# Gates of the gated recurrence: the narrow layers moved between the z products, gate input and last gate layer joined by group, the next attention opened later

## The chip, the cores and the metric

The kernel runs as one program on one core of a Trainium2 chip. The time is the device time of one execution in microseconds. The kernel before took 1679.32 us as the median of three runs (1677.64 to 1679.97). The lines below are of one more execution, taken by the hardware profiler.

The core's engines each have their own queue of instructions and meet only at semaphores. TensorE (PE) multiplies and writes to PSUM, which has eight banks of 128 partitions by 2 KB. ScalarE (ACT) and VectorE (DVE) read PSUM and write to the on-chip memory SBUF. GpSimd (POOL) works on SBUF, and SyncE (SP) issues the DMAs.

## What is computed

Four layers stand one behind the other, on x of 16 sequences of 100 tokens with 256 features and a context of 16 sequences of 361. Layer 0 is a self attention, a cross attention and an MLP with layer norms; layer 1 has two attentions, each with a gated MLP. Layer 2 holds the part that is changed, and layer 3 attends to the context again. Of layer 2, cut to what matters here:

```python
x_norm = _rms(x, norm1_scale)
q = x_norm @ Wq + bq
k = x_norm @ Wk + bk
v = x_norm @ Wv + bv
z = x_norm @ Wz + bz
gamma_base = jax.nn.sigmoid(jax.nn.gelu(z @ Wg1 + bg1) @ Wg2 + bg2)
gamma_mod = jax.nn.sigmoid(jax.nn.gelu(k @ Wgc1 + bgc1) @ Wgc2 + bgc2)
gamma = jnp.clip(gamma_base * gamma_mod, 1e-06, 1.0 - 1e-06)

def step(h_prev, zt_gt):
    z_t, g_t = zt_gt
    gate = jax.nn.sigmoid(z_t @ Wgz + bgz + h_prev @ Wgh + bgh)
    h_tilde = (1.0 - gate) * h_prev + gate * z_t
    h_t = h_tilde + g_t * h_prev
    return (h_t, h_t)
```

The recurrence runs over the 100 tokens. Beside it, the same layer attends with 8 heads from q to the context (mem_k and mem_v are the context), and adds h, the attention's output and 0.1 v.

## The kernel before, in words

Features lie on the partitions, tokens on the free axis: 16 sequences are four groups g of 4, and a group is N = 400 columns. 256 features are two halves m. So a product of one group is one [128 x 400] tile of PSUM for each half, and a weight of 256 x 256 takes two matrix products per half. On TensorE each fp32 product of 400 columns shows as two matmul records; a pair of halves is eight records (x8).

The stages are s0, c0, f0 (layer 0), s1, f1, c1, f2 (layer 1), then the gates, then c2 (the attention of layer 2, with the 100 steps of the recurrence woven in), ft and layer 3. The order on each engine is written out by hand: `program_pe`, `program_act`, `program_dve`, `program_pool` call the same stages, and generators that yield at each slot ("fill", "opening", "step") are advanced with `next` at fixed places, at the same places on every engine. Waits are computed from marks, so an instruction waits for what it reads and for what must be free, and no more.

The stage of the gates is `pe_gates`, `act_gates` and `dve_gates`. Names in it:

- z: the product x_norm Wz (line 777 calls `pe_products`, whose matmuls are line 405); ScalarE adds the bias and writes zs (line 1185).
- ga: the two narrow layers z Wg1 and x_norm (Wk Wgc1), 64 outputs each, side by side in one bank (lines 789 and 790); ScalarE applies the gelu (line 1189, tile GH, which lies in probs).
- gz: the gate input z Wgz (line 793); ScalarE writes it to t (T2, two buffers), and VectorE splits it into three bf16 parts (lines 1624 to 1631, "split").
- gA and gB: the last gate layers (line 801), four matmuls a group; ScalarE applies the sigmoid (lines 1201 and 1202), VectorE multiplies, clips and adds one (lines 1637, 1640, 1643, "gm").
- the opening: what the attention c2 needs before its first sequence (`pe_open`, lines 588 to 612). In slots: two query products q, the keys of sequence 0 (one slot and an empty one), then three slots with the values v of a key chunk and a product "tops" (line 488) whose maxima VectorE takes (line 1343), one with tops alone, the keys of sequence 1 (and an empty slot), and the turn of the maxima (line 496). That makes 11 slots.

The stage runs in three loops over g: all z; then ga, gz and one slot of the opening for each g; then gA, gB and two slots for each g. On VectorE the second loop is the splits, the third the gm's, each with the opening's maxima in the same slots.

PSUM is given out by rings that remember who frees each bank: `flow` (banks 0 to 5) for z, ga, gz, gA and gB, a ring of banks 4 and 6 for q, v and the turn of c2, and pairs (0,1) and (2,3) for keys and tops. A take on TensorE waits for the reader of that bank's last use:

```python
if b + i in freed:
    if due(freed[b + i]):
        pe.wait_ge(producer(freed[b + i]), at(freed[b + i]))
freed[b + i] = point
```

Behind the gates, ScalarE waits for the last gm (line 1208) before it goes on, and GpSimd's first step of the recurrence waits for it too (line 1820). The first step on TensorE (lines 821 and 828) waits for the last split and the last gB, and the first scores R0 (lines 515 and 518) wait for the maxima's rows (line 1354).

## Time and profile before

| | us |
|---|---|
| median of three runs | 1679.32 |
| lowest, highest | 1677.64, 1679.97 |
| time of the profiled execution | 1679.33 |
| its span, first to last instruction | 1677.6 |
| PE busy | 1583.5 (94%) |
| DVE busy | 775.7 (46%) |
| ACT busy | 673.0 (40%) |
| POOL busy | 257.2 (15%) |

The span is 1.73 us shorter than the time of the same execution; the rest lies around it. TensorE is busy nearly all the time, so the places of interest are the few where it isn't. The stage of the gates runs from 1121 to 1190 us of the span. The granted clock of TensorE is a mean of 0.96 of full speed over the whole span.

### The profile page before, as it was taken

To read this page: it belongs to the slowest core of one execution; us is meant where nothing else is said; L and a number is where in the kernel's file an instruction comes from. 1 tells how busy PE (TensorE), PEld (TensorE's weight loads), DVE (VectorE), ACT (ScalarE), POOL (GpSimd) and SP (SyncE) were. 2 spreads that over 40 slices of the span, in tenths; PEclk is the share of its full clock that TensorE was granted. 3 is DMA by queue.
4 is the path that set the end of the run, shared out by engine and by line. 5 is a ranking of instruction groups with operands and counts; after the bars stand their busy time and mean duration, and the time that the engine had idled before them with its cause. 6 is when DMAs were issued, how large, how long until landed. Compare 5 with 4: busy or idle time off the path is not lost.

```text
span 1677.6 us, 30686 instructions
## 1 busy us (share of the span) xinstructions
PE 1583.5 (94%) x13224; PEld 1028.4 (61%) x13224; DVE 775.7 (46%) x1568; ACT 673.0 (40%) x1417; POOL 257.2 (15%) x446
## 2 busy tenths in 40 slices
PE   7998899999999999999999999998899999979998
PEld 6655456666665556555677765553677777645565
DVE  1567767667552245311233332235465566552132
ACT  2455446556454433111234422234453444333343
POOL 1333301010000000000022210000243344320000
PEclk9899989999899999999999999999798799889999
DMA  4211000000000010000100000000000000011021
GB/s 149 97 46 37 19 26 2 2 2 2 2 5 22 0 76 1 19 1 0 76 1 1 1 26 0 0 7 1 26 2 2 2 2 2 2 37 38 0 90 57
DMA packets 19272, 36.97 MB, mean 22 GB/s; under 512 B 2016, under 2 KB 17344, under 8 KB 17856
## 3 DMA queue, kind: packets, MB, share of 16 engines
q1 hardware_dynamic: 19136, 35.01, 6.3%
q8 instruction: 104, 1.70, 0.4%
q14 instruction: 32, 0.26, 0.0%
HBM read 33.36 MB, written 1.64 MB: 21 GB/s over the span
## 4 chain that ended last, share of the span: by engine, by line
PE 84%; DVE 10%; ACT 5%; issue 1%; DMA 0%; SPq 0%; DVEq 0%; ACTq 0%
PE psum L405 37%; PE psum L729 10%; PE psum L518 8%; PE psum L450 8%; PE psum L550 6%; PE psum L488 2%; DVE maxima L1343 2%; PE psum L515 2%; PE psum L828 2%; ACT probs L1026 2%; DVE denoms L1381 1%; PE psum L856 1%; PE psum L869 1%; DVE q_then_o L1386 1%; PE psum L821 1%; PE psum L837 1%
## 5 line engine op out<-in xcount | busy, mean ns | idle before, releaser
L1343 DVE TENSOR_REDUCE maxima<-psum 100x2 f32<-100x722 f32 (+3 forms) x332 | 243.9, 758 | 115.9 <-PE psum L488 95.0
L405 PE MATMUL psum<-x_resid,weights 128*128 128x400 f32 x832 | 292.8, 502 | 4.0 <-ACT probs L1026 1.8
L1026 ACT ACTIVATE probs<-psum 128x800 f32<-128x800 f32 (+3 forms) x240 | 171.7, 747 | 148.8 <-PE psum L518 146.7
L405 PEld LDWEIGHTS psum<-x_resid,weights 128*128 128x128 f32 x832 | 155.7, 190 | 120.3 <-issue 4.3
L729 PE MATMUL psum<-weights 128*128 128x400 f32 x512 | 175.0, 499 | 0.7 <-DVE maxima L1343 0.7
L405 PE MATMUL psum<-weights,ctx_t 128*128 128x256 f32 (+1 forms) x576 | 162.4, 407 | 2.4 <-ACT weights L947 1.7
L450 PE MATMUL psum<-ctx_t,weights 128*128 128x361 f32 x384 | 146.2, 508 | 3.1 <-ACT probs L947 1.3
L729 PEld LDWEIGHTS psum<-weights 128*128 128x128 f32 x512 | 97.2, 190 | 75.1 <-DVE maxima L1343 0.8
L515 PE MATMUL psum<-max_rows,ones_bf 32*128 32x200 bf16 (+7 forms) x1152 | 132.1, 237 | 9.3 <-ACT probs L1026 5.6
L997 ACT ACTIVATE values<-psum 128x256 f32<-128x256 f32 (+2 forms) x176 | 67.5, 384 | 150.9 <-PE psum L405 115.8
L405 PEld LDWEIGHTS psum<-weights,ctx_t 128*128 128x128 f32 (+1 forms) x576 | 101.6, 190 | 41.7 <-issue 9.8
L947 ACT ACTIVATE weights<-psum 128x400 f32<-128x400 f32 (+2 forms) x80 | 38.0, 475 | 210.4 <-PE psum L405 210.3
L550 PE MATMUL psum<-probs,values 128*32 128x100 f32 (+5 forms) x3328 | 115.7, 259 | 0.4 <-DVE q_then_o L1399 0.2
L518 PE MATMUL psum<-q_then_o,keys 32*128 32x100 f32 (+4 forms) x1280 | 109.7, 298 | 0.0
L1773 POOL TENSOR_TENSOR q_masked_bf<-q_then_o,ones 128x200 bf16<-128x200 f32 x48 | 25.5, 535 | 502.8 <-ACT q_then_o L947 439.4
L550 PEld LDWEIGHTS psum<-probs,values 128*32 128x32 f32 (+5 forms) x3328 | 87.7, 117 | 24.1 <-issue 20.9
L1567 DVE TENSOR_TENSOR weights<-psum,weights 128x400 f32<-128x400 f32 x64 | 36.7, 574 | 138.3 <-PE psum L405 120.0
L518 PE MATMUL psum<-q_masked,keys 32*128 32x200 f32 (+2 forms) x1024 | 99.5, 350 | 0.0
L450 PEld LDWEIGHTS psum<-ctx_t,weights 128*128 128x128 f32 x384 | 72.2, 201 | 43.6 <-issue 12.2
L518 PEld LDWEIGHTS psum<-q_then_o,keys 32*128 32x128 f32 (+4 forms) x1280 | 96.0, 191 | 3.0 <-issue 0.5
L947 ACT ACTIVATE weights<-psum,vectors 128x400 f32<-128x400 f32 x80 | 46.3, 592 | 111.4 <-PE psum L405 102.8
L515 PEld LDWEIGHTS psum<-max_rows,ones_bf 32*128 32x128 bf16 (+5 forms) x1152 | 67.1, 120 | 33.3 <-DVE maxima L1343 11.3
(151 smaller groups left out, 2238.2 us busy)
## 6 DMA issues: line engine op xcount, KB each, us to landing
weights<-in_w SPq DMA_DIRECT2D x2, 3072.0 KB, 9.6
staged<-in_ctx SPq DMA_DIRECT2D x32, 128.0 KB, 2.1
values<-in_ctx SPq DMA_DIRECT2D x32, 128.0 KB, 2.2
weights<-in_w SPq DMA_DIRECT2D x3, 1024.0 KB, 4.8
weights<-in_src SPq DMA_DIRECT2D x1, 2368.0 KB, 13.4
weights<-in_w SPq DMA_DIRECT2D x1, 2048.0 KB, 7.8
weights<-in_tw SPq DMA_DIRECT2D x2, 1024.0 KB, 4.8
staged<-in_ctx SPq DMA_DIRECT2D x16, 105.0 KB, 2.1
```

Source lines behind the costliest of these rows:

```text
L405: i = nc.tensor.matmul(PS[0:rows, bk, 0:n], lhs, rhs, start=k == 0, stop=k == len(terms) - 1)
L450: i = nc.tensor.matmul(PS[:, bk + m, 0:C], w(WN[t][1], c, m * P, (m + 1) * P), CT[:, b, c, :], start=c == 0, stop=c == DC - 1)
L488: i = nc.tensor.matmul(PS[0:S, bk + d, 0:C], queries_bf(t, b, i0 + d, c, e), keys_bf(t, b, i0 + d, c), start=True, stop=True)
L515: nc.tensor.matmul(PS[0:kn, bk + d, m * n:(m + 1) * n], ONEB[tile_rows(t, i0 + d), 0:kn], MB[tile_rows(t, i0 + d), b % 2, c * n:(c + 1) * ...
L518: i = nc.tensor.matmul(PS[0:kn, bk + d, m * n:(m + 1) * n], keys_of(t, b, i0 + d, c, k0, kn), queries_of(t, b, i0 + d, c), start=False, st ...
L550: mm = nc.tensor.matmul(PS[tile_rows(t, i), bk, o:o + S], lhs, probs_of(t, b, i, c, kc, kn, e), start=kc == 0, stop=kc == lastk)
L729: i = nc.tensor.matmul(PS[:, bk, 0:N], w(wd, k, m * P, (m + 1) * P), hidden[:, k, :], start=k == 0, stop=k == 7)
L947: nc.scalar.activation(out, PS[0:rows, bank(use), 0:n], func, **kw).then_inc(act_results, mark("act", point or f"{use} out"))
L997: nc.scalar.activation(dst, src, ACT.Copy).then_inc(act_results, mark("act", f"{use} out"))
L1026: nc.scalar.activation(PT[0:kn, k % PROBS_KEPT, :, 0:n], PS[0:kn, bk:bk + 2, 0:n], ACT.Exp).then_inc(act_results, mark("act", f"{t} p{b} { ...
L1343: nc.vector.reduce_max(top, src, AX).then_inc(dve_results, mark("dve", f"{t} m{b} {j}"))
L1567: nc.vector.tensor_tensor(H[:, m, :], PS[:, bank(up), 0:N], U[:, m % 2, :], ALU.mult).then_inc(dve_results, mark("dve", f"{of} u{g} {m}"))
```

## The change

The amount of work stays the same; its order changes, on TensorE, ScalarE and VectorE alike.

1. The narrow layers ga of group g - 1 follow the z products of group g; those of the last group follow gz of group 0 (`pe_gate_downs`).
2. The second and the third loop become one: gz of g, then gA and gB of g, and on VectorE the split of g, then gm of g.
3. The table OPEN_AT says how many slots of the opening are advanced: none in the loop of z; after gz of group g 0, 1, 2, 4; after gA and gB of group g 0, 1, 4, 1. So no slot is used at group 0, both queries come at group 1, the keys of sequence 0 and all values and tops at group 2, and the keys of sequence 1 and the turn at group 3, ahead of its gA and gB.
4. VectorE advances both numbers of a group at once, between its split and its gm.

```diff
--- before.py
+++ after.py
@@ -150,6 +150,8 @@
 AFTER = {"f0": "c0", "f1": "s1", "f2": "c1", "ft": "c2"}
 NORM_AFTER = {"f0": "n3", "f2": "r1"}
 TAIL_AT = 10
+
+OPEN_AT = ((0, 0, 0, 0), (0, 1, 2, 4), (0, 1, 4, 1))
 OPENS = {"f0": "s1", "f1": "c1"}
 PROBS_KEPT = 6
 ROUND_AT = {}
@@ -580,6 +582,10 @@
             for _ in itertools.zip_longest(*parts):
                 yield
 
+        def advance(part, slots):
+            for _ in range(slots):
+                next(part, None)
+
         def later(slots, part):
             for _ in range(slots):
                 yield
@@ -764,6 +770,17 @@
             for m in range(DC):
                 pe_products(pe, lin[""], f"bias {name}{m}", f"bias {name}{m} out", [(w(ww, k, m * P, (m + 1) * P), vec(bv, k)) for k in range(DC)], n=1)
 
+        def pe_gate_downs(pe, g):
+
+            for m in range(DC):
+                if due(f"z{g} {m} out"):
+                    pe.wait_ge(act_results, at(f"z{g} {m} out"))
+            bk = flow.take(pe, f"ga{g}", f"ga{g} out")
+            for k in range(DC):
+                nc.tensor.matmul(PS[0:64, bk, 0:N], w("wg1", k, 0, 64, 64), seq("zs")[:, k, cols(g)], start=k == 0, stop=k == DC - 1)
+                i = nc.tensor.matmul(PS[64:P, bk, 0:N], w("k2", k, 0, 64, 64), XN[g][:, k, :], start=k == 0, stop=k == DC - 1)
+            i.then_inc(products_ready, mark("pe", f"ga{g}"))
+
         def pe_gates(pe):
 
             opening = pe_open(pe, "c2")
@@ -780,19 +797,15 @@
                     if due("w c2"):
                         pe.wait_ge(producer("w c2"), at("w c2"))
                     pe_bias(pe, "o2", "awo", "abv")
+                else:
+                    pe_gate_downs(pe, g - 1)
+                advance(opening, OPEN_AT[0][g])
             for g in range(NG):
                 for m in range(DC):
-                    if due(f"z{g} {m} out"):
-                        pe.wait_ge(act_results, at(f"z{g} {m} out"))
-                bk = flow.take(pe, f"ga{g}", f"ga{g} out")
-                for k in range(DC):
-                    nc.tensor.matmul(PS[0:64, bk, 0:N], w("wg1", k, 0, 64, 64), seq("zs")[:, k, cols(g)], start=k == 0, stop=k == DC - 1)
-                    i = nc.tensor.matmul(PS[64:P, bk, 0:N], w("k2", k, 0, 64, 64), XN[g][:, k, :], start=k == 0, stop=k == DC - 1)
-                i.then_inc(products_ready, mark("pe", f"ga{g}"))
-                for m in range(DC):
                     pe_products(pe, flow, f"gz{g} {m}", f"gz{g} {m} out", [(w("gz", k, m * P, (m + 1) * P), seq("zs")[:, k, cols(g)]) for k in range(DC)])
-                next(opening, None)
-            for g in range(NG):
+                if g == 0:
+                    pe_gate_downs(pe, NG - 1)
+                advance(opening, OPEN_AT[1][g])
                 if due(f"ga{g} out"):
                     pe.wait_ge(act_results, at(f"ga{g} out"))
                 for m in range(DC):
@@ -800,8 +813,7 @@
                         bk = flow.take(pe, f"{name}{g} {m}", f"{name}{g} {m} out")
                         nc.tensor.matmul(PS[:, bk, 0:N], WT[rows, WAT[ww] + m * P:WAT[ww] + (m + 1) * P], GH[rows, g, :],
                                          start=True, stop=True).then_inc(products_ready, mark("pe", f"{name}{g} {m}"))
-                next(opening, None)
-                next(opening, None)
+                advance(opening, OPEN_AT[2][g])
             for _ in opening:
                 pass
 
@@ -1185,23 +1197,25 @@
                     act_evac(act, f"z{g} {m}", seq("zs")[:, m, cols(g)], bias=vec("bz", m))
                 if g == 0:
                     act_root(act, "r1", NG - 1)
+                else:
+                    act_evac(act, f"ga{g - 1}", GH[:, g - 1, :], func=ACT.Gelu_apprx_tanh, bias=vec("d_gates"))
+                advance(opening, OPEN_AT[0][g])
             for g in range(NG):
-                act_evac(act, f"ga{g}", GH[:, g, :], func=ACT.Gelu_apprx_tanh, bias=vec("d_gates"))
                 given = f"gz split{g - 2}" if g >= 2 else f"r1 t{NG - 2 + g} 1"
                 if due(given):
                     act.wait_ge(dve_results, at(given))
                 for m in range(DC):
                     act_evac(act, f"gz{g} {m}", T2[:, g % 2, m, :], bias=vec("d_gz", m))
-                next(opening, None)
-            for g in range(NG):
+                if g == 0:
+                    act_evac(act, f"ga{NG - 1}", GH[:, NG - 1, :], func=ACT.Gelu_apprx_tanh, bias=vec("d_gates"))
+                advance(opening, OPEN_AT[1][g])
                 if g >= 2:
                     if due(f"gm{g - 2}"):
                         act.wait_ge(dve_results, at(f"gm{g - 2}"))
                 for m in range(DC):
                     act_evac(act, f"gA{g} {m}", seq("gms")[:, m, cols(g)], func=ACT.Sigmoid, bias=vec("bg2", m))
                     act_evac(act, f"gB{g} {m}", SG[:, g % 2, m, :], func=ACT.Sigmoid, bias=vec("bgc2", m))
-                next(opening, None)
-                next(opening, None)
+                advance(opening, OPEN_AT[2][g])
             for _ in opening:
                 pass
             if due(f"gm{NG - 1}"):
@@ -1617,6 +1631,7 @@
             nc.vector.memset(HP[:, :, :, :], 0.0).then_inc(dve_results, mark("dve", "hp0"))
             mark_same("h-1", "hp0")
             mark_same("wp2", "hp0")
+            advance(opening, sum(OPEN_AT[0]))
             for g in range(NG):
                 if due(f"gz{g} 1 out"):
                     dve.wait_ge(act_results, at(f"gz{g} 1 out"))
@@ -1629,8 +1644,7 @@
                 if due(f"gz rest {g}"):
                     dve.wait_ge(dve_results, at(f"gz rest {g}"))
                 nc.vector.tensor_tensor(parts[:, :, 2, :], gz, parts[:, :, 1, :], ALU.subtract).then_inc(dve_results, mark("dve", f"gz split{g}"))
-                next(opening, None)
-            for g in range(NG):
+                advance(opening, OPEN_AT[1][g] + OPEN_AT[2][g])
                 if due(f"gB{g} 1 out"):
                     dve.wait_ge(act_results, at(f"gB{g} 1 out"))
                 gm = seq("gms")[:, :, cols(g)]
@@ -1641,8 +1655,6 @@
                 if due(f"clip{g}"):
                     dve.wait_ge(dve_results, at(f"clip{g}"))
                 nc.vector.tensor_scalar(gm, gm, 1.0, None, ALU.add).then_inc(dve_results, mark("dve", f"gm{g}"))
-                next(opening, None)
-                next(opening, None)
             for _ in opening:
                 pass
 
```

In the rows of order below, x4 means four instructions alike, and what an instruction waits for stands in brackets. The changed file has 12 lines more above this place, so its line numbers are higher.

TensorE, the end of the gates, before, from the last tops (line 488) to the first step of the recurrence (821). Line 801 is gA and gB, 450 the keys of sequence 1, 496 the turn:

```order
L488 MATMUL psum<-keys_bf,q_masked_bf 100x361 [waits dve_results]
L488 MATMUL psum<-keys_bf,q_masked_bf 100x361
L801 MATMUL psum<-probs,weights 128x400 [waits dve_results]
L801 MATMUL psum<-probs,weights 128x400 x3
L450 MATMUL psum<-ctx_t,weights 128x361 [waits act_results]
L450 MATMUL psum<-ctx_t,weights 128x361 x3
L801 MATMUL psum<-probs,weights 128x400 x4
L496 MATMUL psum<-constants,maxima 128x100
L821 MATMUL psum<-weights,ident_bf 128x96 [waits act_results]
```

The same place in the changed kernel: 490 is tops, 407 on weights the gate input gz of the last group, 452 the keys of sequence 1, 498 the turn, 814 gA and gB:

```order
L490 MATMUL psum<-keys_bf,q_masked_bf 100x361 [waits dve_results]
L490 MATMUL psum<-keys_bf,q_masked_bf 100x361
L490 MATMUL psum<-keys_bf,q_masked_bf 100x361 [waits dve_results]
L490 MATMUL psum<-keys_bf,q_masked_bf 100x361
L407 MATMUL psum<-weights 128x400 [waits dve_results]
L407 MATMUL psum<-weights 128x400 x3
L452 MATMUL psum<-ctx_t,weights 128x361 [waits act_results]
L452 MATMUL psum<-ctx_t,weights 128x361 x3
L498 MATMUL psum<-constants,maxima 128x100 [waits dve_results]
L814 MATMUL psum<-probs,weights 128x400 x4
L833 MATMUL psum<-weights,ident_bf 128x96 [waits act_results,dve_results]
```

The gA and gB of group 2 no longer stand between the tops and the keys; gz of group 3 does. Only one set of gA and gB is left behind the tops, and it follows the turn. The tops and gz wait for VectorE's maxima.

VectorE, from the last split to the start of the second gm, before. Lines 1624 to 1631 are a split, 1637 to 1643 a gm, 1343 the maxima:

```order
L1624 CAST weights<-t 128x2x400 [waits act_results]
L1627 TENSOR_TENSOR weights<-t,weights 128x2x400 [waits dve_results]
L1628 TENSOR_TENSOR t<-t,weights 128x800
L1631 TENSOR_TENSOR weights<-t,weights 128x2x400 [waits dve_results]
L1637 TENSOR_TENSOR weights<-weights,probs 128x2x400 [waits act_results]
L1640 TENSOR_SCALAR weights<-weights 128x2x400 [waits dve_results]
L1643 TENSOR_SCALAR weights<-weights 128x2x400 [waits dve_results]
L1343 TENSOR_REDUCE maxima<-psum 100x2 [waits products_ready] x2
L1637 TENSOR_TENSOR weights<-weights,probs 128x2x400 [waits act_results]
```

The same engine in the changed kernel, from the split of group 2 (1639 to 1646) over all maxima (1357) and the gm of group 2 (1651 to 1657) to the split of group 3:

```order
L1639 CAST weights<-t 128x2x400 [waits act_results]
L1642 TENSOR_TENSOR weights<-t,weights 128x2x400 [waits dve_results]
L1643 TENSOR_TENSOR t<-t,weights 128x800
L1646 TENSOR_TENSOR weights<-t,weights 128x2x400 [waits dve_results]
L1357 TENSOR_REDUCE maxima<-psum 100x2 [waits products_ready] x4
L1651 TENSOR_TENSOR weights<-weights,probs 128x2x400 [waits act_results]
L1654 TENSOR_SCALAR weights<-weights 128x2x400 [waits dve_results]
L1657 TENSOR_SCALAR weights<-weights 128x2x400 [waits dve_results]
L1639 CAST weights<-t 128x2x400 [waits act_results]
```

Before, the splits of all groups come ahead of the first gm, and that gm ahead of the first maxima. Now two gm's are done by then, and the maxima stand ahead of the third.

ScalarE, before, from the z of group 1 on. A result in weights is zs or a sigmoid, one in probs is a gelu or a sigmoid, one in t is gz:

```order
L947 ACTIVATE weights<-psum,vectors 128x400 [waits products_ready] x6
L947 ACT_TABLE_LOAD
L947 ACTIVATE probs<-psum,vectors 128x400 [waits products_ready]
L947 ACTIVATE t<-psum,vectors 128x400 [waits products_ready] x2
L947 ACTIVATE q_then_o<-psum,vectors 128x400 [waits products_ready]
L947 ACTIVATE probs<-psum,vectors 128x400 [waits products_ready]
```

In the changed kernel:

```order
L959 ACTIVATE weights<-psum,vectors 128x400 [waits products_ready] x2
L959 ACT_TABLE_LOAD
L959 ACTIVATE probs<-psum,vectors 128x400 [waits products_ready]
L959 ACTIVATE weights<-psum,vectors 128x400 [waits products_ready] x2
L959 ACTIVATE probs<-psum,vectors 128x400 [waits products_ready]
L959 ACTIVATE weights<-psum,vectors 128x400 [waits products_ready] x2
L959 ACTIVATE probs<-psum,vectors 128x400 [waits products_ready]
L959 ACTIVATE t<-psum,vectors 128x400 [waits products_ready] x2
L959 ACTIVATE probs<-psum,vectors 128x400 [waits products_ready]
L959 ACT_TABLE_LOAD
L959 ACTIVATE weights<-psum,vectors 128x400 [waits products_ready]
```

The table of the gelu is loaded behind the second group's z. The table of the sigmoid is loaded behind the last gelu, as before; what now follows that gelu at once is the first sigmoid.

## Rows read from the trace of the kernel before

**Rows 1.** Page, the chain that ended last, shares of the span by engine

```profile
PE 84%; DVE 10%; ACT 5%; issue 1%; DMA 0%; SPq 0%; DVEq 0%; ACTq 0%
```

**Rows 2.** Windows: start:end, length; busy (records) of PE, PEld, DVE, ACT, POOL; clock; DMA; GB/s

```profile
1134.00:1158.00 24.00, 22.21 (x80) 10.18 (x79) 10.91 (x12) 11.62 (x19) 1.82 (x2) 1.00 0.00 1
1158.00:1187.00 29.00, 20.65 (x68) 9.63 (x66) 13.09 (x17) 13.18 (x25) 0.00 (x0) 0.76 0.00 0
1166.00:1170.00 4.00, 2.65 (x8) 1.18 (x8) 2.11 (x3) 0.92 (x2) 0.00 (x0) 0.66 0.00 0
1194.00:1198.00 4.00, 3.21 (x32) 2.51 (x31) 2.21 (x10) 1.21 (x3) 0.90 (x5) 0.50 0.00 0
1360.00:1380.00 20.00, 19.63 (x254) 13.81 (x250) 10.58 (x38) 6.95 (x21) 5.36 (x13) 1.00 0.01 2
1420.00:1440.00 20.00, 20.00 (x201) 15.14 (x201) 9.69 (x36) 6.91 (x21) 6.95 (x15) 0.58 0.00 1
```

**Rows 3.** Timeline of TensorE: start, duration in us; in brackets idle before, releaser

```profile
1129.85 5.54 PE L405 MATMUL psum<-staged,weights 128*128 128x400 f32 x16
1135.32 0.55 PE L789 MATMUL psum<-weights 128*64 128x400 f32 x1
...
1136.81 2.95 PE L405 MATMUL psum<-weights 128*128 128x400 f32 x8
...
1151.90 2.70 PE L450 MATMUL psum<-ctx_t,weights 128*128 128x361 f32 x8 [0.69 <-ACT t L947]
...
1162.74 1.13 PE L405 MATMUL psum<-weights,ctx_t 128*128 128x256 f32 x4 [1.04 <-ACT weights L947]
...
1163.80 0.35 PE L488 MATMUL psum<-keys_bf,q_masked_bf 32*100 32x361 bf16 x2
...
1167.35 3.04 PE L801 MATMUL psum<-probs,weights 64*128 64x400 f32 x8 [1.85 <-DVE maxima L1343]
...
1179.72 4.94 PE L450 MATMUL psum<-ctx_t,weights 128*128 128x361 f32 x8 [1.25 <-ACT probs L947]
...
1184.59 1.61 PE L801 MATMUL psum<-probs,weights 64*128 64x400 f32 x8
...
1187.73 0.34 PE L821 MATMUL psum<-weights,ident_bf 128*128 128x96 bf16 x1 [1.29 <-ACT probs L947]
...
1190.25 0.21 PE L515 MATMUL psum<-max_rows,ones_bf 32*128 32x100 bf16 x2 [1.60 <-DVE max_rows L1354]
```

**Rows 4.** Groups by line, TensorE: busy us, mean ns, idle before and its releasers

```profile
L801 PE MATMUL psum<-probs,weights 64*128 64x400 f32 x32 | 9.3, 716 | 4.8 <-DVE maxima L1343 4.8
```

**Rows 5.** Timeline of VectorE in the gates

```profile
1140.43 0.58 DVE L1624 CAST weights<-t 128x800 bf16<-128x800 f32 x1 [6.55 <-ACT t L947]
...
1142.97 0.99 DVE L1631 TENSOR_TENSOR weights<-t,weights 128x800 bf16<-128x800 f32 x1
...
1166.39 1.72 DVE L1343 TENSOR_REDUCE maxima<-psum 100x2 f32<-100x722 f32 x2
...
1187.70 0.99 DVE L1637 TENSOR_TENSOR weights<-weights,probs 128x800 f32<-128x800 f32 x1 [5.88 <-ACT probs L947]
...
1189.34 0.58 DVE L1643 TENSOR_SCALAR weights<-weights 128x800 f32<-128x800 f32 x1
...
1190.11 0.25 DVE L1655 TENSOR_REDUCE scan_state<-psum 128x32 f32<-128x96 f32 x1
```

**Rows 6.** Timeline of ScalarE in the gates

```profile
1136.04 1.28 ACT L947 ACT_TABLE_LOAD   x1
1137.33 0.59 ACT L947 ACTIVATE probs<-psum,vectors 128x400 f32<-128x400 f32 x1
...
1185.62 0.59 ACT L947 ACTIVATE weights<-psum,vectors 128x400 f32<-128x400 f32 x1
...
1187.07 0.60 ACT L947 ACTIVATE probs<-psum,vectors 128x400 f32<-128x400 f32 x1
```

**Rows 7.** Timeline of GpSimd in the gates

```profile
1147.54 1.82 POOL L1773 TENSOR_TENSOR q_masked_bf<-q_then_o,ones 128x200 bf16<-128x200 f32 x2 [162.11 <-ACT q_then_o L947]
```

## The prediction

> **What bounds the kernel now.** I read the page first: the chain that ended last lies on TensorE for 84% of the span and on VectorE and ScalarE for 15% [rows 1]. So the change matters where TensorE waits or runs slowly. Then I cut the stage of the gates into windows [rows 2]. From 1134 to 1158 us TensorE is busy 22.21 of 24 us at clock 1.00; from 1158 to 1187 it is busy 20.65 of 29 us at clock 0.76. The second loop is nearly dense, the third isn't. The timeline of TensorE [rows 3] and its groups [rows 4] say why. The matmuls of gA and gB wait 4.8 us in all for VectorE's maxima; once it is 1.85 us, at 1167.35. The order says what those maxima stood behind: the last split and the first gm. The maxima free the bank pairs that the next gA needs, so TensorE waits for work of VectorE that it does not need itself. In those waits the clock falls: 0.66 from 1166 to 1170 with TensorE busy 2.65 of 4 us [rows 2]. At 1.2 GHz eight records of gA and gB take 3.04 us and not 1.61, and the keys' eight 4.94 and not 2.70 [rows 3].
>
> What ends last in the stage is a chain over three engines. TensorE ends the last gB at 1184.59 + 1.61 = 1186.2; ScalarE's last sigmoid ends at 1187.07 + 0.60 = 1187.67 [rows 6]; the last gm runs from 1187.70 to 1189.34 + 0.58 = 1189.92 [rows 5]; the first sum of the recurrence starts at 1190.11, and the first scores R0 at 1190.25, after 1.60 us of waiting for the maxima's rows [rows 3].
>
> **What the same work needs without waits.** The change adds and removes no matmul, evacuation, vector operation or DMA, and it leaves the number of table loads alone: the order shows one for the gelu and one for the sigmoid. So I price TensorE's work from 1135.32, where the z products end before, each group at clock 1.00 [rows 3]:
> - four narrow layers at 1136.81 - 1135.32 = 1.49: 5.96
> - four gz at the price of a z pair, (1135.32 - 1129.85) / 2 = 2.74: 10.96
> - two queries, half of that, 1.37: 2.74
> - two times keys at 2.70: 5.40
> - three v at 1163.80 - 1162.74 = 1.06: 3.18
> - four tops and the turn at 0.35 (the turn has no row here; it is one transpose, and I give it the price of tops): 1.75
> - four times gA and gB at 1.61: 6.44
>
> Sum 36.4, so that the last gB could end at 1171.75. It ends at 1186.2. Of the 14.5 us between, 4.8 are the waits of [rows 4], 0.69, 1.04 and 1.25 are three other waits of [rows 3], 2 x (3.04 - 1.61) = 2.9 (two of the four sets of gA and gB ran so) and 4.94 - 2.70 = 2.2 are the slow clock. The rest, 1.6, is smaller gaps that I don't list. All the z come in the same place as before; the three narrow layers between them run in banks long free, and each follows the z of a later group, so that ScalarE has had 2.74 us for an evacuation of 0.59 us [rows 6]. No wait there.
>
> **The waits that the new order brings.** I walked the three queues with the rings of banks.
> - gA of group 1 takes the bank of the query just issued, and waits until ScalarE has emptied it. The keys at 1151.90 waited 0.69 for just such an evacuation [rows 3]. I take 0.7.
> - The first v waits for the first sigmoid of group 2, which stands behind four evacuations of keys. The v before waited 1.04 at 1162.74 [rows 3], with a table load in front; without one I get 0.2. Bounds 0 and 1.04.
> - gz of group 3 takes the pair of the third tops and waits for their maxima. v with tops takes 1.06 + 0.35 = 1.41, a maximum 1.72 / 2 = 0.86 [rows 5], so VectorE keeps up, and only the last one shows: 0.86. I take 0.9. Bound below 0, above 1.85, the wait in [rows 3].
> - The keys of sequence 1 take the pair of gz and wait for both its evacuations: 0.7 again.
> - The turn waits for the fourth maximum, done long before (gz and keys, 5.4 us, lie between), and behind the turn stand gA and gB of group 3. Nothing.
> - The masks of GpSimd, 1.82 us for two [rows 7], start when the second query is out; before the first tops there lie gz, keys and gA with gB, 2.74 + 2.70 + 1.61 = 7 us. Nothing.
>
> Sum 2.5, so the last gB ends at 1174.25. Behind it the pieces are those of before in the same order: ScalarE has keys to empty, then four sigmoids, and ends 1187.67 - 1186.2 = 1.47 later: 1175.7. The last gm takes 1189.92 - 1187.70 = 2.22: 1177.95. The maxima's rows now lie ahead of it, so the first sum starts at 1178.0, and not at 1190.11. That is 12.1 us less.
>
> Is VectorE free enough? Its first split can start when gz of group 0 is emptied: 1135.32 + 3 x 1.49 + 2.74 + 0.75 = 1143.3, 2.9 later than the 1140.43 of before. From there it has four splits of 1142.97 + 0.99 - 1140.43 = 3.53, four gm of 2.22, four maxima of 0.86 [rows 5], and one operation for the maxima's rows that I give 0.86 too, an upper bound: 27.3. It would be done at 1170.6, 7.4 us ahead of the end I found. It has that much to spend on waits; a wait of 5.88 stood ahead of the last gm before [rows 5].
>
> What follows moves as a whole: the recurrence and R0 start from the last gm, the last split, the maxima's rows and the last sigmoid, and all come 12 us earlier. No load is late: the next weights (f1 of the tail) are issued when the last gB ends, as before, and are wanted only behind the whole of c2.
>
> A rule of the Trainium skill, ScalarE: Activation LUTs, section What ACT_TABLE_LOAD costs, speaks against part of this: it gives 1283 ns for the load plus about 1380 ns of drain for a switch. In this trace the load takes 1.28 us and the activation behind it starts 0.01 us after its end, 1136.04 + 1.28 against 1137.33 [rows 6], so no drain stands behind the load. By the rule the sigmoids of group 0 would come 1.38 us later, the first query's evacuation some 0.5 later, and the gain would be an estimated 11.6; by the rows it is 12.1.
>
> **The sum.** The span is 1677.6 and the same execution's time 1679.33, which is the median's 1679.32 within 0.01; 1.73 us lie around the span. 1677.6 - 12.1 + 1.73 = 1667.2 us. For this case alone I give 1665.5 to 1669.
>
> **The rivals.**
> - *The clock falls inside the new order.* It fell before with TensorE busy 2.65 of 4 us. In the new order it is busy 36.4 of 38.9 us, 94%, as in the dense window (22.21 of 24, 93%, clock 1.00) [rows 2]; but the tops and their maxima stand close together, and the waits of 0.9 and 0.7 with them. If it falls at the third tops, gz (2.74 x (4.94 / 2.70 - 1) = 2.3), keys (2.2) and gA with gB (1.4) grow: 5.9 lost, gain 6.2, 1673.1 us.
> - *The clock stays up at the start of c2.* From 1194 to 1198 it is 0.50 with TensorE busy 3.21 of 4 us [rows 2], after the waits ahead of the first scores. Those are shorter now. At full clock the 3.21 would be 1.6, over ten us of such a stretch 4.0; the steps' chain over VectorE and ScalarE does not quicken, so 2 to 3. Gain 14.6, 1664.7 us.
> - *The change doesn't do what it says.* The maxima were put ahead of gm and gz behind maxima, so the chain third maximum, gz, wait, keys, turn, gA with gB, sigmoids, gm (2.74 + 0.7 + 2.70 + 0.35 + 1.61 + 1.47 + 2.22 = 11.8) ends the stage. I have the third maximum end at 1166.2. If VectorE's queue (split, gm, split, gm, split, four maxima) gets there only at 1178, nothing is gained: 1679 us. For it: VectorE's two kinds of work now alternate, each waiting for ScalarE. Against: 7.4 us of slack, and each group's data are there 3 us or more ahead.
> - *Slower: the slow clock spreads in c2.* From 1420 to 1440 the clock is 0.58 and TensorE gets through 201 records; from 1360 to 1380 at 1.00 it is 254, in both cases busy nearly all of 20 us [rows 2]. Such a stretch costs (254 - 201) / 254 x 20 = 4.2 us. The stage starts 12 us earlier and meets the clock's changes elsewhere. It decides from three more such stretches on (12.6, against a gain of 12.1); with four it is 1684 us. Against: the three runs differ by only 2.33 us, less than one stretch.
>
> **How the numbers follow.** The forecast 0.58, clock falls in the gates 0.18, clock stays up 0.12, other sizes of the same gain 0.04, no gain 0.05, slower 0.03. A measurement of this kernel can tell about 0.2%, 3.4 us, from no change. The first four are faster: 0.92; same 0.05; slower 0.03. The range 1663.5 to 1673.5 takes in both cases of the clock and the bounds of the four waits (1.0 less, or 1.8 more).
>
> **What would show it.** In the changed profile, the last gB should end near 1174, the last gm near 1178, and the first scores follow without a wait for the maxima's rows. The waits of gA and gB for maxima (4.8) should be gone, and one of about 0.9 stand ahead of the last gz. The clock should be 1.00 from 1134 to 1174, with eight records of gA and gB at 1.61 in all groups. The splits should start near 1143, and the sigmoid's table be loaded once. I am wrong if the last gm ends after 1184, if the sigmoids trail TensorE by much more than 1.5 us, or if the time between the first sum and the end of the span grows by more than 3 us.

## The result, and the profile after

| | before | after |
|---|---|---|
| median of 4 runs, us | 1678.48 | 1661.22 |
| lowest, highest | 1677.62, 1679.97 | 1659.63, 1662.4 |
| profiled execution: time, span | 1679.33, 1677.6 | 1661.62, 1659.9 |
| mean granted clock of TensorE | 0.960 | 0.966 |

The changed kernel takes 0.9896 of the time before, 95% interval 0.9878 to 0.9913: faster by 17.3 us. I had forecast 12.1 us less and a range down to 1663.5, so the direction was right and the size was not: 5 us more came than the walk through the gates gives, and 1661.22 lies below the range.

To see where the time went, cut both spans at three marks: VectorE's first scaling of v2 (the first operation behind the norm), the first of the hundred sums of the recurrence and the last of them.

| us | before | after | difference |
|---|---|---|---|
| start to first scaling of v2 | 1130.4 | 1129.5 | -0.9 |
| gates: to the first sum | 59.7 | 47.7 | -12.0 |
| c2: to the hundredth sum | 292.6 | 288.0 | -4.6 |
| rest of the span | 194.9 | 194.7 | -0.2 |

Two rows give the last three marks: VectorE's sums by their line, with least, median and longest duration in ns, then the start of the first and of the last. Before:

```profile
L1655 DVE TENSOR_REDUCE scan_state<-psum x100: 246/257/259, 1190.1 to 1482.7; 128x32 f32<-128x96 f32 x100
```

After:

```profile
L1667 DVE TENSOR_REDUCE scan_state<-psum x100: 247/258/259, 1177.2 to 1465.2; 128x32 f32<-128x96 f32 x100
```

So the gates came out as worked out, and the rest of the gain lies in c2, whose instructions the change does not touch. First the page of after, busy time and the shares of the chain:

```profile
PE 1574.6 (95%) x13224; PEld 1023.7 (62%) x13224; DVE 774.5 (47%) x1568; ACT 673.4 (41%) x1417; POOL 257.3 (16%) x446
PE 84%; DVE 10%; ACT 4%; issue 1%; DMA 0%; SPq 0%; POOL 0%; DVEq 0%; ACTq 0%; POOLq 0%
```

TensorE has the same 13224 records and is busy 8.9 us less (1583.5 before): the same work ran at a higher clock for part of the time. Its gate layers as one group, to set beside [rows 4]:

```profile
L814 PE MATMUL psum<-probs,weights 64*128 64x400 f32 x32 | 7.0, 525 | 0.7 <-ACT q_then_o L959 0.7
```

The mean record fell from 716 to 525 ns, the idle time before the group from 4.8 us behind maxima to 0.7 behind a query. TensorE's timeline over the second half of the new order, beside [rows 3] (start, length, engine, line, operation, wait in brackets):

```profile
1150.18 1.61 PE L814 MATMUL psum<-probs,weights 64*128 64x400 f32 x8 [0.68 <-ACT q_then_o L959]
...
1158.38 2.11 PE L814 MATMUL psum<-probs,weights 64*128 64x400 f32 x8
...
1165.52 2.95 PE L407 MATMUL psum<-weights 128*128 128x400 f32 x8 [0.97 <-DVE maxima L1357]
1169.25 2.67 PE L452 MATMUL psum<-ctx_t,weights 128*128 128x361 f32 x8 [0.78 <-ACT t L959]
1171.76 0.25 PE L498 MATMUL psum<-constants,maxima 100*128 100x100 f32 x1
1171.94 1.61 PE L814 MATMUL psum<-probs,weights 64*128 64x400 f32 x8
1175.16 0.34 PE L833 MATMUL psum<-weights,ident_bf 128*128 128x96 bf16 x1 [1.61 <-ACT probs L959]
```

The four waits that I had put at 0.7, 0.2, 0.9 and 0.7 are 0.68, 0.50 (inside the 2.11 of group 2: eight records alone take 1.61), 0.97 and 0.78, 2.9 us against 2.5. The last gB ends at 1173.55, for 1174.25 in the forecast, with the stage starting 0.9 earlier. The closing stretch on VectorE, beside [rows 5]:

```profile
1164.55 1.73 DVE L1357 TENSOR_REDUCE maxima<-psum 100x2 f32<-100x722 f32 x2 [0.42 <-PE psum L490]
...
1172.59 0.36 DVE L1368 TENSOR_TENSOR max_rows<-psum,constants 128x200 bf16<-128x200 f32 x1
1175.05 0.99 DVE L1651 TENSOR_TENSOR weights<-weights,probs 128x800 f32<-128x800 f32 x1 [2.11 <-ACT probs L959]
1176.08 0.58 DVE L1654 TENSOR_SCALAR weights<-weights 128x800 f32<-128x800 f32 x1
1176.69 0.58 DVE L1657 TENSOR_SCALAR weights<-weights 128x800 f32<-128x800 f32 x1
1177.18 0.25 DVE L1667 TENSOR_REDUCE scan_state<-psum 128x32 f32<-128x96 f32 x1
```

VectorE now waits 2.11 us for the last sigmoid, and its row of maxima was ready long before. The first scores start at 1175.93, without a wait for that row. Last, the clock by windows (length, busy time and records of PE, PEld, DVE, ACT and POOL, then the granted clock, DMA share, GB/s), two of the gates and then c2:

```profile
1134.00:1158.00 24.00, 23.32 (x86) 11.28 (x82) 12.71 (x16) 13.81 (x25) 1.46 (x2) 1.00 0.00 1
1158.00:1174.00 16.00, 13.80 (x55) 7.03 (x53) 11.52 (x15) 8.67 (x19) 0.00 (x0) 1.00 0.00 1
1177.20:1214.78 37.58, 35.51 (x409) 26.53 (x406) 20.64 (x82) 17.22 (x47) 15.31 (x36) 0.78 0.02 7
1245.09:1288.86 43.77, 42.47 (x499) 30.97 (x499) 23.29 (x85) 15.32 (x45) 13.92 (x33) 0.81 0.01 2
1288.86:1320.06 31.20, 30.45 (x468) 23.40 (x467) 21.57 (x83) 15.15 (x45) 13.93 (x33) 1.00 0.01 2
1402.57:1417.98 15.41, 15.30 (x245) 12.01 (x245) 11.36 (x43) 7.80 (x23) 7.45 (x17) 1.00 0.01 3
1438.35:1465.23 26.88, 26.14 (x365) 20.78 (x368) 15.10 (x59) 9.21 (x29) 9.51 (x24) 0.68 0.01 2
1177.20:1465.20 288.00, 278.26 (x3828) 209.42 (x3828) 181.98 (x679) 125.61 (x367) 116.27 (x274) 0.91 0.01 3
```

The stretches of c2 are cut at the same steps of the recurrence in both kernels: 0 to 12, 24 to 36, 36 to 48, 78 to 84, 90 to 99, then the whole. The same of before:

```profile
1190.10:1225.70 35.60, 34.13 (x425) 26.06 (x426) 21.16 (x81) 17.15 (x47) 15.25 (x36) 0.86 0.01 5
1256.02:1297.18 41.16, 39.69 (x499) 28.86 (x499) 23.91 (x84) 15.19 (x45) 13.90 (x33) 0.88 0.01 2
1297.18:1335.36 38.18, 37.54 (x468) 28.64 (x467) 21.52 (x82) 15.35 (x45) 13.88 (x33) 0.78 0.01 2
1417.87:1440.28 22.41, 22.41 (x245) 17.27 (x247) 11.34 (x42) 8.00 (x23) 7.45 (x17) 0.62 0.00 1
1460.65:1482.64 21.99, 19.64 (x362) 15.38 (x365) 15.37 (x58) 9.18 (x29) 9.48 (x24) 1.00 0.01 3
1190.10:1482.70 292.60, 281.92 (x3848) 212.03 (x3852) 183.31 (x680) 125.82 (x367) 116.00 (x274) 0.91 0.01 2
```

Steps 0 to 12 take 2.0 us more after, 24 to 36 take 2.6 more, 36 to 48 take 7.0 less, 78 to 84 take 7.0 less, 90 to 99 take 4.9 more: together 4.5 less, of c2's 4.6. In each pair of rows the records agree within 5% and the longer one has the lower clock. The steps in between (12 to 24, 48 to 78, 84 to 90) take the same time in both to 0.02 us. Of the 4.6 us, 3.7 are busy time of TensorE (281.92 to 278.26) and 0.9 idle time. The change moved the places at which TensorE runs at its lower level, 1.2 GHz, and in before they lie where they cost more.

### The profile page after: what moved, and what is told of

It reads as the page before. It is cut to its first block, busy times and chain, and to the rows that moved or that the text cites. A ratio compares the mean times of both kernels' runs of the same rounds, so it can differ in the third digit from the quotient of the medians.

```text
span 1659.9 us, 30691 instructions
## 1 busy us (share of the span) xinstructions
PE 1574.6 (95%) x13224; PEld 1023.7 (62%) x13224; DVE 774.5 (47%) x1568; ACT 673.4 (41%) x1417; POOL 257.3 (16%) x446
## 4 chain that ended last, share of the span: by engine, by line
PE 84%; DVE 10%; ACT 4%; issue 1%; DMA 0%; SPq 0%; POOL 0%; DVEq 0%; ACTq 0%; POOLq 0%
PE psum L407 38%; PE psum L735 10%; PE psum L520 8%; PE psum L452 8%; PE psum L552 6%; PE psum L490 2%; DVE maxima L1357 2%; PE psum L517 2%; PE psum L840 2%; ACT probs L1038 2%; DVE denoms L1395 1%; PE psum L868 1%; PE psum L881 1%; DVE q_then_o L1400 1%; PE psum L833 1%; PE psum L849 1%
```

## The experiments

They ask two things: which part of the change makes the 12 us, and why c2, untouched, got shorter. Kernels are named by what they change; each table entry below is of the profiled execution unless it says median. The ratio and its 95% interval are estimated from all runs of a comparison, with before measured beside them, and need not be the quotient of the medians.

### Both kernels again

No edit. Was the c2 of each kernel an accident of one execution?

> The kernel before, unchanged, as a second measurement. The change gained 17.3 us of median where I had worked out 12.1; its stage of the gates gave just that 12.1, the rest came from c2, the attention behind the gates. Theory A (the clock's slow stretches in c2 lie elsewhere from execution to execution, and the four runs of each kernel happened to differ): this kernel's c2, from the first sum of the recurrence to the hundredth, will be 3 us or more off the 290 of the first profile, or the median more than 2 us off 1678.5. Theory B (how the gates end decides how c2 runs, the same way in each execution): first sum near 1190, c2 within 1.5 us of the first profile, median 1677.5 to 1680.

> The changed kernel, unchanged, with more runs. Its gates gained 12.0 us, the median 17.3; joined loops with an early opening gained 9.3 in the gates and 15.7 in the median, the late opening alone 13.8 and 21.0. Theory A (the slow stretches of c2 are drawn anew in each execution and the rest of the gain is chance of few runs): with more runs the median moves to 1664 or above, 1678.4 less 12.1 being 1666.3, and the runs spread over 10 us or more, as those of the kernel before do (1667 to 1689). Theory B (kernels whose gates end without waits have a shorter c2): the median stays at 1660 to 1662.5.

| | gates | c2 | rest | median us (runs) | ratio to before |
|---|---|---|---|---|---|
| before again | 59.7 | 292.6 | 194.9 | 1678.54 (12) | 1.0004 [0.9979, 1.0029] |
| after again | 47.8 | 288.0 | 194.7 | 1660.23 (4) | 0.9880 [0.9860, 0.9899] |

From the start of the gates on both repeat to 0.1 us in every stage; that start came at 1130.0 in before (1130.4 the first time) and at 1127.5 in after (1129.5). The lower clock stands at the same steps as in the first execution: in before at 1 to 4, 27 to 30, 40 to 44 and 79 to 83; in after at 0 to 5, 27 to 31 and 92 to 97. So the 4.6 us are no accident of one execution. After's median stayed where it was, so more runs did not bring it to the 1664 of the first theory either. One thing is new: the twelve runs spread from 1670.08 to 1686.52. Beside the other kernels before ran 77 times more: 9 times between 1667.3 and 1673.6, 48 times between 1676.8 and 1680.5, 20 times between 1681.2 and 1696. The steps between these clumps are near the 7.0 us of one stretch above, and the clock goes with them: the mean granted clock of a run is 0.965 on average in the lowest clump, 0.961 in the middle one and 0.956 in the highest. The first three runs, 2.33 us apart, had shown only the middle clump. After's eight runs lie within 1659.63 to 1662.4.

### The narrow layers alone

```diff
-            for g in range(NG):   # ga at the head of the loop of gz
-                ... wait for z of g; ga of g
+                # in the loop of z: behind z of g, ga of g - 1
+                else:
+                    pe_gate_downs(pe, g - 1)
+            for g in range(NG):
+                if g == 1:
+                    pe_gate_downs(pe, NG - 1)
```

> The kernel before with the first part alone: the narrow layers between the z products, those of the last group behind gz of group 0; the loops of gz and of gA and gB stay apart and the opening stays where it was. My theory (the loss is VectorE's splits and gm's ahead of the maxima, and the narrow layers' place only removes a wait of about 1 us): first sum 0 to 1.5 us earlier than before, median 1677 to 1679. Rival (the narrow layers' place carries the change, since ScalarE's evacuations of z and gelu lie beside TensorE's work): first sum 5 us earlier or more, median under 1674.

Gates 57.4 (2.3 less), median 1676.87 of 12 runs, ratio 0.9990 [0.9969, 1.0011]: no difference that can be told. The first sum came at 1196.0, later and not earlier than in before, since the stage began only at 1138.6. In this execution c2 took 283.3. If most runs had that c2 and began the gates near 1130, the median would be near 1666; it isn't, so in most of them one or the other was different. The group of the gate layers shows why the gates gained so little:

```profile
L808 PE MATMUL psum<-probs,weights 64*128 64x400 f32 x32 | 7.9, 619 | 4.8 <-DVE maxima L1353 4.8
```

The 4.8 us of waits for maxima stand as before. What is gone is the wait of 1.10 us ahead of a narrow layer (at 1155.70 in before), and one set of records ran at full clock (619 ns for 716).

### The late opening alone

```diff
+LATE = (0, 2, 6, 3)
 # loop of gz:
-                next(opening, None)
 # loop of gA, gB (and gm):
-                next(opening, None)
-                next(opening, None)
+                advance(opening, LATE[g])
```

> The kernel before with the late opening alone: narrow layers and the three loops as before, no slot of the opening in the loop of gz, and 0, 2, 6, 3 slots behind gA and gB of groups 0 to 3; the maxima stand behind the third gm. My theory (what TensorE lost were waits for maxima that stood behind splits and gm's; a late opening lets the splits finish beside gz and the narrow layers): the gates gain 8 to 13 us, first sum at 1177 to 1182 (less up to 1 us by where the stage starts), median 1663 to 1670. Rival (the loops must be joined, since only so the last gm has no other gm's ahead of it): first sum not before 1186, median 1674 or more.

Gates 45.9, that is 13.8 less, where the whole change has 12.0 and I had expected 8 to 13; median 1657.44 of 5 runs, ratio 0.9863 [0.9839, 0.9888], below the 1663 to 1670 expected and below after. The loops stand as in before, only the opening's slots come later:

```profile
L806 PE MATMUL psum<-probs,weights 64*128 64x400 f32 x32 | 7.2, 528 | 1.2 <-DVE maxima L1345 0.7 <-ACT weights L951 0.4 <-ACT values L1001 0.2
```

And its end on TensorE:

```profile
1170.06 0.94 PE L806 MATMUL psum<-probs,weights 64*128 64x400 f32 x4 [0.69 <-DVE maxima L1345]
1170.93 2.70 PE L452 MATMUL psum<-ctx_t,weights 128*128 128x361 f32 x8
1173.47 0.25 PE L498 MATMUL psum<-constants,maxima 100*128 100x100 f32 x1
1173.56 0.34 PE L825 MATMUL psum<-weights,ident_bf 128*128 128x96 bf16 x1
```

Here the keys of sequence 1 (2.70) come behind the last gB and run while ScalarE and VectorE finish the gates, so no wait stands ahead of the turn or the first step (825). In after they come ahead of the last gA, and TensorE waits 1.61 us ahead of the first step, at 1175.16.

### The joined loops with the opening early

The narrow layers stay between the z products here too.

```diff
-OPEN_AT = ((0, 0, 0, 0), (0, 1, 2, 4), (0, 1, 4, 1))
+OPEN_AT = ((0, 0, 0, 0), (1, 1, 1, 1), (2, 2, 2, 1))
```

> The changed kernel with its opening early: slots 1, 1, 1, 1 behind gz and 2, 2, 2, 1 behind gA and gB, as many as before at like places; narrow layers between the z and joined loops stay. If the joined loops carry the gain, the first sum comes within 2 us of the change's 1177.2 and the median within 3 us of 1661. If the late opening carries it, maxima wait behind splits and gm's again, the first sum comes at 1183 or later, and the median is 1667 or more.

Gates 50.4 (9.3 less than before, 2.7 more than after), c2 285.9, median 1662.66 of 6 runs, ratio 0.9911 [0.9885, 0.9937]. First sum (1178.1) and median fall as I had written for the case that the joined loops carry the gain; the first sum hides 1.8 us of the difference, since this stage began that much sooner than after's.

```profile
L814 PE MATMUL psum<-probs,weights 64*128 64x400 f32 x32 | 6.5, 522 | 0.9 <-ACT q_then_o L959 0.7 <-ACT values L1009 0.2
```

In the gate layers no wait for maxima is left here (0.7 with the late opening); the largest wait of the stage, 2.47 us ahead of the first step, is for VectorE's last split. So the joined loops (9.3, with the 2.3 of the narrow layers' place perhaps among them) and the late opening (13.8) remove the same waits, and together they make 12.0, not 23. Joined loops without the moved narrow layers were not run.

### Late opening and narrow layers, loops apart

The edit is the two of above together.

> The run with the late opening alone, and the narrow layers between the z products besides (those of the last group behind gz of group 0). Late opening alone: gates 45.9 us, median 1657.4. My theory (the narrow layers' place is worth the one wait it removed under the early opening, and that wait is gone already): gates 45 to 47 us, median 1656 to 1660. Rival (the two parts add up: 2.3 us more, as the narrow layers gave alone): gates 43.6 us, median under 1655.5. Third case: VectorE, whose splits of 3.5 us now follow products of 2.8 us, becomes late: gates 47 us or more.

Gates 46.0, c2 286.6, median 1658.8 of 5 runs, ratio 0.9889 [0.9860, 0.9919]. The narrow layers' 2.3 us don't come on top of the 13.8 of the late opening. And the loops needn't be joined: these gates are 1.7 us shorter than after's 47.7. That difference need not be a cost of the joined loops: the next kernel keeps them joined, changes the place of the keys of sequence 1, and gets below both.

### The keys of sequence 1 behind the last gate layer

```diff
-OPEN_AT = ((0, 0, 0, 0), (0, 1, 2, 4), (0, 1, 4, 1))
+OPEN_AT = ((0, 0, 0, 0), (0, 1, 2, 0), (0, 1, 4, 5))
 # VectorE, behind the gm of group g:
-                advance(opening, OPEN_AT[1][g] + OPEN_AT[2][g])
+                if g + 1 < NG:
+                    advance(opening, OPEN_AT[1][g] + OPEN_AT[2][g])
```

> The changed kernel with the keys of sequence 1 and the turn behind gA and gB of the last group and not ahead of them, and on VectorE the last gm ahead of the maxima's rows. In the changed kernel's trace the last sigmoid ends 2.5 us behind TensorE's last gB, since four evacuations of keys stand ahead, and gz, wait, keys, turn and gates follow one another. My theory: gA and gB come right behind gz at 1168.4, the sigmoids end at 1171.9, the last split at 1172.7 is then the latest, gm ends at 1174.9, and the rows follow the turn: first sum at 1175.2, 2 us earlier than the change's 1177.2 (gates 45.7 us against 47.7), median 1.5 to 2.5 us lower than the changed kernel's of the same job. Rival (the keys' place gives nothing, since the first scores then wait for keys and rows): first sum within 0.7 of 47.7, median the same.

Gates 45.5, median 1656.08 of 4 runs, ratio 0.9851 [0.9827, 0.9876]: the lowest of all, 4.2 us below after in the same comparison, where I had expected 1.5 to 2.5 (the two sets of four runs don't overlap, the intervals of the ratios just do). Late opening alone, in another comparison, is 1.4 above it, too close to tell. Of the spans, 1654.4 against 1658.0, the gates give 2.3, c2 (285.8) 2.2 and the rest behind it (191.9) 2.8, while the part ahead of the stage is 3.7 longer; only the gates' share is the edit's own mechanism. TensorE:

```profile
1167.23 2.95 PE L407 MATMUL psum<-weights 128*128 128x400 f32 x8 [0.97 <-DVE maxima L1357]
1170.12 1.61 PE L814 MATMUL psum<-probs,weights 64*128 64x400 f32 x8
1171.66 2.70 PE L452 MATMUL psum<-ctx_t,weights 128*128 128x361 f32 x8
...
1176.84 0.22 PE L517 MATMUL psum<-max_rows,ones_bf 32*128 32x100 bf16 x2 [1.48 <-DVE max_rows L1368]
```

VectorE:

```profile
1174.30 0.98 DVE L1652 TENSOR_TENSOR weights<-weights,probs 128x800 f32<-128x800 f32 x1
1175.32 0.58 DVE L1655 TENSOR_SCALAR weights<-weights 128x800 f32<-128x800 f32 x1
1175.93 0.58 DVE L1658 TENSOR_SCALAR weights<-weights 128x800 f32<-128x800 f32 x1
1176.42 0.36 DVE L1368 TENSOR_TENSOR max_rows<-psum,constants 128x200 bf16<-128x200 f32 x1
1176.70 0.25 DVE L1668 TENSOR_REDUCE scan_state<-psum 128x32 f32<-128x96 f32 x1
```

The gA and gB of the last group follow gz at once, so VectorE no longer waits for the last sigmoid (2.11 in after) and runs without a gap from the last split to the first sum. VectorE is what ends the stage now.

### Why c2 got shorter: the moment it begins, or the waits ahead of it

After with the first sum put back to about where before has it, in two ways. With TensorE busy, by products whose result is overwritten:

```diff
+            for _ in range(18):
+                nc.tensor.matmul(PS[:, SCAN_BANK, 0:N], w("awo", 0, 0, P), X[:, 0, cols(0)], start=True, stop=True)
             for t in range(S):
```

> The changed kernel with 18 more products of 128x400 fp32 on TensorE (36 records) between the gates and the first step of the recurrence; their result is not used. They cost 18 x 0.684 = 12.3 us of TensorE, of which about 1.5 to 2 lie beside the last gm: the first sum comes 10.5 to 11 us later, near 1188, where that of the kernel before came, but with TensorE busy and at full clock all the way. Theory A: c2 as in any execution, median 10.5 to 11 us above that of the changed kernel. Theory B in the form that only waits ahead of c2 lengthen it: the same, 10.5 to 11. Theory C (it is the moment at which c2 starts that matters): c2 as before, 292 us, median 15 us or more above the changed kernel.

With TensorE waiting, by eleven operations of VectorE ahead of the last step of the last gm:

```diff
+                if g == NG - 1:   # cut: the waits and marks between the eleven
+                    for n in range(11):
+                        nc.vector.tensor_tensor(T2[:, 0], T2[:, 0], T2[:, 0], ALU.max)
                 nc.vector.tensor_scalar(gm, gm, 1.0, None, ALU.add)
```

> The changed kernel with 11 operations of VectorE on 128x800 ahead of the last operation of the last gm, their result not used: 11 x 1.0 = 11 us in which TensorE waits behind its first scores. The first sum comes 11 us later, near 1188, as in the run with 18 more products, but with TensorE idle and at the low clock when c2 goes on. Theory A: median 11 us above the changed kernel, 1 more for the low clock at the start. Theory B (waits ahead of c2 lengthen it): c2 5 us longer or more than with the 18 products, median 15 us or more above the changed kernel.

| | gates | first sum | c2 | median us (runs) | ratio to before |
|---|---|---|---|---|---|
| after again | 47.8 | 1175.3 | 288.0 | 1660.23 (4) | 0.9880 |
| busy by 18 products | 58.6 | 1197.1 | 285.2 | 1671.17 (8) | 0.9939 [0.9916, 0.9962] |
| idle by 11 operations | 58.9 | 1191.5 | 287.6 | 1669.14 (11) | 0.9952 [0.9934, 0.9969] |

One of the eight runs with products took 5204.18 us and stands outside all others, for a reason that nothing here shows; without it the median is 1670.92. Both c2 are shorter than before's 292.6, though c2 begins later than in before (1190.1), and one has 11 us of waiting ahead of it. Over after's 1660.23 the medians are 10.7 and 8.9 higher, about as much as the gates (10.8 and 11.1) or less. The theory of the moment wanted 15 or more with the products, the theory of the waits 15 or more with the idle time, and neither came. So a late start of c2 does not make it long by itself, and the c2 behind 11 us of waiting is only 2.4 us longer than the other. An exact match of the moment was not tested: the first sums came 7.0 and 1.4 us behind before's. A guess is left: before's own order meets the lower clock in bad places, and nearly any shift frees it.

### A small push to before

That can be tried: before, with its gates as they are, and 2, 4 or 8 of the same products ahead of the first step. If the order of before is an unlucky one, added work makes it faster.

```diff
+            for _ in range(4):   # 2, 4, 8
+                nc.tensor.matmul(PS[:, SCAN_BANK, 0:N], w("awo", 0, 0, P), X[:, 0, cols(0)], start=True, stop=True)
             for t in range(S):
```

> The kernel before with 2 more products of 128x400 fp32 on TensorE, result not used, ahead of the first step of the recurrence: 1.37 us, and TensorE waits 1.60 us there for the maxima's rows, so that first sum and first scores stay where they are (gates 59.7 to 59.9 us) and only TensorE's activity and the moment of its small matmuls change. Theory L (in the kernel before, the low clock in the gates ties the clock's changes to the work, so that nearly all executions go through c2 with the same unlucky slow stretches, at steps 40 and 79; a small push ahead of c2 unties them): c2 288 us or less and the median 3 us or more under that of the kernel before. Rival R (c2 of the kernel before is long for a reason that a push does not touch): c2 292 to 293, median within 1.5 us of before.

> The same with 4 more products, 2.74 us, of which 1.6 are hidden: gates 60.8 us. Theory L: c2 288 us or less, median 2 us or more under before although work is added. Rival R: median 1 us above before, c2 292 to 293.

> The same with 8 more products, 5.5 us, of which 1.6 are hidden: gates 63.6 us. Theory L: c2 288 us or less, median between 1 us under and 1 us above before. Rival R: median 4 us above before, c2 292 to 293.

| products added | gates | c2 | median us (11 runs each) | ratio to before |
|---|---|---|---|---|
| 0 (before, 27 runs) | 59.7 | 292.6 | 1678.93 | |
| 2 | 59.7 | 290.1 | 1673.87 | 0.9978 [0.9953, 1.0003] |
| 4 | 60.8 | 285.2 | 1672.07 | 0.9968 [0.9943, 0.9992] |
| 8 | 63.5 | 284.7 | 1672.29 | 0.9966 [0.9942, 0.9990] |

With four products, whole c2 and steps 36 to 48:

```profile
1188.80:1474.00 285.20, 275.83 (x3849) 207.61 (x3850) 182.40 (x679) 125.42 (x367) 115.56 (x272) 0.93 0.01 2
1296.11:1327.31 31.20, 30.34 (x484) 23.44 (x483) 22.20 (x84) 15.09 (x45) 13.88 (x33) 1.00 0.01 2
```

Two needed a c2 of 288 or less to fit and have 290.1, a miss; their median is 5.1 us lower, but the interval of the ratio takes in 1. Four hit in both. Eight hit in c2 and gained more than the theory had: 6.6 us of median, where I had at most 1. Added work made the kernel faster, by 6.9 us of median with four; the ratio gives 5.4, and its interval 1.3 to 9.6. With four, steps 36 to 48 take 31.20 us at full clock, to the hundredth what they take in after, for 38.18 in before.

The tables leave out one stage, ahead of the gates: from the start of the span to the first scaling of v2. No edit touches it, and yet it took 1127.5 to 1131.2 us in ten of the fourteen profiled executions, and more in four: 1132.6 (idle by 11 operations), 1136.6 (two products), 1138.5 (18 products) and 1138.6 (narrow layers alone). From the first product of line 496 to the first of line 515, before and the kernel with two products:

```profile
31.25:45.71 14.46, 14.46 (x94) 13.54 (x95) 3.40 (x15) 3.51 (x10) 0.00 (x0) 0.95 0.11 24
32.53:52.05 19.52, 19.52 (x95) 17.57 (x95) 3.40 (x15) 3.51 (x10) 0.00 (x0) 0.70 0.09 18
```

The same records, busy throughout, take 5.1 us more at the lower mean clock; that is most of the 6.2 us between these two starts. So a step of some 7 us between two runs can come from here as well as from c2. It bears on the test above: the profiled executions with 18 products (1678.67), with 11 operations (1675.92) and with two products (1682.61) lie 7 to 9 us above the medians of their kernels, and their c2 comes behind an unusual start.

## Why the prediction was right in the gates and wrong in the total

- *TensorE's walk, 36.4 us of work and 2.5 of waits.* Right: waits of 2.9, last gB 0.7 us before the forecast with the stage 0.9 early. The waits were sized with some luck: I took 1.85 us as the largest for maxima, but before has a larger one that my rows left out, and the bound above should have been that. The one in question came out at 0.97.

```profile
1175.43 3.04 PE L801 MATMUL psum<-probs,weights 64*128 64x400 f32 x8 [2.97 <-DVE maxima L1343]
```

- *The waits of gA and gB for maxima go.* Right, 4.8 to 0; what reappears is the 0.97 ahead of the last gz, forecast at 0.9. The rival that the change does not do what it says, in which VectorE gets to the maxima too late, fell with it.
- *The clock stays at 1.00 in the new order.* Right: both windows of the gates show 1.00, with TensorE busy 23.32 of 24 and 13.80 of 16 us. Together that is 93%, against 94% forecast; the second alone is 86%, and the clock held nevertheless. The splits start at 1142.89, for "near 1143".
- *No drain behind the sigmoid table's load.* Right. ScalarE in after:

```profile
1143.77 0.59 ACT L959 ACTIVATE probs<-psum,vectors 128x400 f32<-128x400 f32 x1 [0.91 <-PE psum L781]
1144.39 1.28 ACT L959 ACT_TABLE_LOAD   x1
1145.68 0.59 ACT L959 ACTIVATE weights<-psum,vectors 128x400 f32<-128x400 f32 x1
```

  The load starts 0.03 us after the last gelu's end, and the sigmoid 0.01 us after the load's. The Trainium skill, ScalarE: Activation LUTs, What ACT_TABLE_LOAD costs, adds some 1380 ns of drain to a load of 1283 ns. This trace agrees on the load (1.28 us) and has no room for the drain on either side of it. My estimate of the gain by the Trainium skill was 11.6; the gates give 12.0.
- *Sigmoids 1.47 and gm 2.22 behind the last gB.* Right: last gB ends 1173.55, gm begins 1175.05, the first sum 1177.18: from last gB to first sum 3.63 us, for 3.75 in the forecast (1174.25 to 1178.0).
- *"What follows moves as a whole."* This is the step that failed. The first sum came 12.0 us earlier relative to the stage's start, as forecast, but c2 then took 288.0 for 292.6, and the stage began 0.9 sooner. Had c2 been rigid, the profiled execution would have taken 1661.62 + 4.6 = 1666.2, a microsecond from the forecast. I had weighed two rivals of the clock in c2. "The clock stays up at the start" named the right cause in the wrong place: steps 0 to 12 got slower by 2.0 us, and the gain came from 36 to 48 and 78 to 84. "The slow clock spreads" had too low a price, 4.2 us for a stretch of 20 from rows with different work in them, where the same steps 78 to 84 differ by 7.0; and it had only a sign against the kernel: I had not asked whether before itself was dear. The rows for that were at hand, 1420 to 1440 at 0.58 with TensorE busy all the time [rows 2]. That c2 moved in the kernel's favour is luck: nothing in the edit aims at it, and 2, 4 or 8 idle products shortened before's c2 too.
- *The range.* The three runs of before, 2.33 us apart, were taken as proof that such stretches do not come and go. 77 runs show steps near 7 us in the time, with the mean clock falling as the time rises. A range of one stretch to either side, 1660 to 1674, would have been what the rows supported.

What is shown, and what is not. Shown: the gates give 12.0 us, and the late opening alone removes nearly all waits of the gate layers for maxima, as do the joined loops with the narrow layers moved. c2 repeats in both kernels to 0.1 us where the gates start within 2 us of each other; it differs between 283.3 and 292.6 in one execution each of twelve programs with the same c2, and before has the longest; four or eight products ahead of it make before faster. Not shown: by what rule the clock falls where it does. That before's waits in the gates (where its clock fell at 1167 and at 1174, and after's did not) set the phase of what follows is argued alone: the kernels with a late opening, whose gate layers wait 0.7 us for maxima or not at all, have 285.8 to 288.0, but the narrow layers alone, with all those waits, have 283.3. Nor is it known how c2 looked in runs without a profile, or why the clock ahead of the gates differs between executions.

## What to carry to other kernels

Where an engine's later work is started early, look at what it puts ahead of the banks that the bottleneck waits for; the same instructions opened later gave 13.8 us here. Letting 2.70 us of keys run under the helper engines' tail took 2.3 us off the gates of the changed kernel. A walk of the queues by rows gave the gates' gain to 0.1 us here (the single waits to 0.3), but a stage near TensorE's clock changes is not a rigid block: cut it at marks of equal work, look for low granted clock at full busy share, and give the range one such stretch each way. Mark the start of the changed stage as well, since what lies ahead of it moved by 11 us with no edit. Before believing that a gain near 1% comes from the edit alone, push the kernel before with a few idle products: here that took 5 to 7 us off the median, where the change took 17.

## What the runs showed of the hardware that I had not expected

- TensorE's granted clock can be low with the engine busy all the time: steps 78 to 84 of before, 22.41 of 22.41 us busy at a mean clock of 0.62. The same 245 records take 15.41 us at 1.00 in after.
- Four added products (eight records started between 1185.3 and 1187.8, gates 1.1 us longer) took 6.9 us off the median (5.4 by the ratio, interval 1.3 to 9.6).
- The same program runs in clumps about 7 us apart (1667 to 1674, 1677 to 1681, 1681 and up), while after keeps within 2.8 us over eight runs. Other late orders had single runs farther off: 1668.22 for a median of 1658.8.
- Ahead of the edit, 94 to 95 like records took 14.46 us in one execution and 19.52 in another, busy throughout, at mean clocks of 0.95 and 0.70.
